# Layer normalisation moved from VectorE to ScalarE, turns of three dense layers reordered, gate softmax once per layer

## The reference, cut to what matters

```python
def _layernorm(x, axis=-1, eps=1e-05):
    m = jnp.mean(x, axis=axis, keepdims=True)
    v = jnp.var(x, axis=axis, keepdims=True)
    return (x - m) / jnp.sqrt(v + eps)

x = x + 0.5 * _L0_ffn_ref(_layernorm(x), ...)     # 128 -> 64 channels -> relu of 16 per channel -> 64 -> 128
x = x + _L0_attn_ref(_layernorm(x), ...)          # 16 heads of 8, rotary, causal
x = x + 0.5 * _L0_ffn_ref(_layernorm(x), ...)
x = x + 0.5 * _L1_ffn_ref(_layernorm(x), ...)     # gate softmax over 8 experts, each takes its top 128 rows
x = x + _L1_attn_ref(_layernorm(x), ...)          # gated recurrence over the 512 rows
x = x + 0.5 * _L1_ffn_ref(_layernorm(x), ...)
```

## Time and profile before

| | us |
|---|---|
| median of 3 runs (lowest to highest) | 1874.82 (1872.78 to 1875.02) |
| the profiled execution, its own time | 1875.22 |
| its span in the trace | 1873.2 |
| busy: PE / DVE / ACT / POOL | 1581.5 / 1360.9 / 1089.0 / 760.4 |
| granted TensorE clock, mean | 0.915 |
| query layer, from its first statistics at | 20.0 |
| attention, first maximum and last score product | 273.6 to 894.5 |
| gate layer, first statistics to last probabilities | 907.9 to 1063.0 |
| scan layer, first statistics to last probabilities | 1399.3 to 1536.3 |
| experts (both), first and last selection matrix | 1123.5, 1864.2 |

### The profile page before, as it was taken

How to read it: one execution, slowest core, us unless ns; L and a number is a source line. 1 busy time by engine, 2 the same in 40 slices (tenths; PEclk the granted TensorE clock), 3 DMA queues, 4 the chain that set the end, 5 groups by cost and what they waited for, 6 DMA issues and landing times. The chain is left out here.

```text
span 1873.2 us, 39185 instructions
## 1 busy us (share of the span) xinstructions
PE 1581.5 (84%) x11698; PEld 1107.9 (59%) x11698; DVE 1360.9 (73%) x3422; ACT 1089.0 (58%) x2225; POOL 760.4 (41%) x1170
## 2 busy tenths in 40 slices
PE   4878749999999999998699529999977751999998
PEld 1444424555555555554355329999964531999997
DVE  4898746777777777774388668777768976777776
ACT  2444313666666666666466427787755531877876
POOL 1565542333333333333233256665401212666540
PEclk9989856999999999999899759999988875999999
DMA  5111231111111111110011301111000110121110
GB/s 135 31 38 50 59 105 36 43 43 42 41 41 41 44 39 42 40 35 2 1 34 33 110 19 39 38 34 29 25 1 23 34 34 12 39 60 46 43 48 23
DMA packets 72819, 76.39 MB, mean 41 GB/s; under 512 B 13040, under 2 KB 61488, under 8 KB 72752
## 3 DMA queue, kind: packets, MB, share of 16 engines
q1 hardware_dynamic: 64560, 58.77, 10.9%
q0 software_dynamic: 8192, 16.79, 3.4%
HBM read 51.40 MB, written 24.12 MB: 40 GB/s over the span
## 5 line engine op out<-in xcount | busy, mean ns | idle before, releaser
L951 DVE TENSOR_REDUCE at_negmax<-at_s_ps 128x2 f32<-128x1024 f32 (+3 forms) x384 | 394.5, 1045 | 174.9 <-PE at_s_ps L741 170.4
L862 ACT ACTIVATE at_p<-at_x_ps 128x512 f32<-128x512 f32 x640 | 353.5, 591 | 224.1 <-PE at_x_ps L751 221.3
L918 POOL TENSOR_SCALAR_AFFINE_SELECT at_p<-at_p 128x256 f32<-128x256 f32 (+1 forms) x448 | 190.7, 438 | 354.9 <-ACT at_p L862 354.9
L1175 POOL DMA_INDIRECT e_x_in<-xn,e_row_c x256 | 258.5, 1010 | 145.7 <-POOL e_row_c L1171 103.5
L739 PE MATMUL at_s_ps<-at_kr,at_qr 72*128 72x512 bf16 (+3 forms) x1024 | 253.0, 312 | 20.6 <-DMA at_kr<-k_parts 18.2
L751 PE MATMUL at_x_ps<-at_qr,at_kr 74*128 74x512 bf16 (+3 forms) x1024 | 236.4, 306 | 23.0 <-ACT at_p L862 12.9
L1296 DVE TENSOR_TENSOR e_hid_lo<-e_hid,e_hid_hi 128x512 fp32r<-128x512 f32 x256 | 177.2, 693 | 85.3 <-ACT e_hid_hi L1260 85.3
L741 PE MATMUL at_s_ps<-maskb,identb 128*128 128x128 bf16 x1024 | 202.1, 225 | 0.0
L1259 ACT ACTIVATE e_hid<-e_h_ps 128x512 f32<-128x512 f32 x256 | 155.0, 605 | 39.4 <-PE e_h_ps L1201 38.9
L766 PE MATMUL at_o_ps<-at_p,at_va 128*32 128x512 f32 (+3 forms) x2048 | 157.0, 449 | 1.6 <-POOL at_p L918 1.6
L1201 PE MATMUL e_h_ps<-e_x_hi,w_hi 128*128 128x256 f32 x512 | 156.0, 305 | 0.1
(11 more groups left out here) (184 smaller groups left out, 3515.2 us busy)
## 6 DMA issues: line engine op xcount, KB each, us to landing
at_qr<-q_parts SPq DMA_DIRECT2D x192, 96.0 KB
k_parts<-m_kparts SPq DMA_DIRECT2D x48, 96.0 KB
at_kr<-k_parts SPq DMA_DIRECT2D x64, 72.0 KB
xres<-in_x_dram SPq DMA_DIRECT2D x8, 512.0 KB, 7.3
xn<-m_n_xhat SPq DMA_DIRECT2D x16, 256.0 KB, 2.3
e_x_in<-xn,e_row_c POOLq DMA_INDIRECT x256, 2.5
xn<-sc_n_xhat SPq DMA_DIRECT2D x16, 256.0 KB, 2.3
out_dram<-xres SPq DMA_DIRECT2D x16, 256.0 KB, 2.3
```

Of the source, the lines that this page charges most:

```text
L862: a.activation(p_sb[g % 2][:, i, :], x_ps[i % 2][:], ACT.Exp, scale=SCALE).then_inc(x_read, 1)
L918: sel = gp.affine_select(out=part, in_=part, compare_op=ALU.is_ge, fill=0.0, base=0, pattern=[[0, n] for n in part.shape[1:-1]] + [[1, P]] ...
L951: v.tensor_reduce(negmax[u][:, h0:h0 + len(heads), c], s_ps[k % 2][:, 0:len(heads) * pitch].rearrange("p (j w) -> p j w", w=pitch)[:, :, 0:w],
L1175: nc.gpsimd.indirect_dma_start(out=x_in[k][u][:], out_offset=None, in_=xn_dram, in_offset=bass.IndirectOffsetOnAxis(ap=row_c[k][:, u:u + 1 ...
```

## The change

1. `Norm.apply` moves from DVE to ACT: `Identity` with scale and bias columns. For the bias POOL multiplies the negated mean (`less`, made by DVE) by the reciprocal deviation (`shift`), behind the power.
2. The pipeline has a fourth stage, `ahead`: statistics, power and shift of norm 1 are made one turn before the head that uses them. `widen` waits until the last pair's normalised rows are done, since the columns have one buffer. In the query and gate layers ACT does norm 1 first in the head's turn; in the scan layer last in the turn before.
3. The turns of the gate and the scan layer are reordered on every engine; the scan layer is written out in full (`unrolled`), with two buffers for `ts`. In the gate layer `g_ps` and `xt2_ps` use other banks, and `HV["gate"]` goes from 3 to 5, so that DVE makes five hidden rows of eight.
4. DVE only copies the scores of a pair (`keep`); maximum, difference, exponential, sum, reciprocal and product are made once at the end of the layer over all 64 groups of 8.

```diff
-HV = {"qkv": 5, "gate": 3}
+HV = {"qkv": 5, "gate": 5}
...
+    def widen(self, dve, i):
+        after(dve, self.xhat_done, i * W)
         dve.wait_ge(self.mv_done, i + 1)
-        v.tensor_scalar(self.vare[:], self.mv[:, :, 1], EPS, None, ALU.add).then_inc(self.var_done, 1)
+        dve.sem_inc(self.dve_turn, 1)
+        self.nc.vector.tensor_scalar(self.less[:], self.mv[:, :, 0], -1.0, None, ALU.mult)
+        self.nc.vector.tensor_scalar(self.vare[:], self.mv[:, :, 1], EPS, None, ALU.add).then_inc(self.var_done, 1)
...
+        pool.wait_ge(self.rstd_done, i + 1)
+        pool.sem_inc(self.pool_turn, 1)
+        self.nc.gpsimd.tensor_tensor(self.shift[:], self.less[:], self.rstd[:], ALU.mult).then_inc(self.shift_done, 1)
+
+    def apply(self, act, i):
+        act.wait_ge(self.shift_done, i + 1)
         for b in range(W):
             for c in range(C):
                 j = b * C + c
-                s = self.nc.vector.tensor_scalar(
+                s = self.nc.scalar.activation(
                     self.xhat[b][:, c * D:(c + 1) * D], self.xres[:, i * W + b, c * D:(c + 1) * D],
-                    self.mv[:, j, 0:1], self.rstd[:, j:j + 1], ALU.subtract, ALU.mult)
+                    ACT.Identity, bias=self.shift[:, j:j + 1], scale=self.rstd[:, j:j + 1])
             s.then_inc(self.xhat_done, 1)
...
+    def keep(self, dve, i):
+        dve.wait_ge(self.scored, (i + 1) * W)
+        self.nc.vector.tensor_copy(self.probs[:, :, bass.ds(i * W * E, W * E)].rearrange("p c (b e) -> p b c e", b=W),
+                                   self.bank[:, 0:W * C * E].rearrange("p (b c e) -> p b c e", b=W, c=C)).then_inc(self.read, 1)
...
+        dve.wait_ge(self.read, TURNS)
+        v.tensor_reduce(self.mx[:], self.each, AX.X, ALU.max).then_inc(self.maxed, 1)
+        dve.wait_ge(self.maxed, 1)
+        v.tensor_tensor(self.each, self.each, self.mx[:].unsqueeze(2).to_broadcast([P, C * NB, E]), ALU.subtract).then_inc(self.lessened, 1)
+        dve.wait_ge(self.exp_done, 1)
+        v.tensor_reduce(self.den[:], self.each, AX.X, ALU.add).then_inc(self.summed, 1)
...
+    turn(0, None, None, None)
+    turn(1, 0, None, None)
+    turn(2, 1, 0, None)
+    turn(3, 2, 1, 0)
+    with eng.Fori(0, TURNS - 4) as r:
+        turn(r + 4, r + 3, r + 2, r + 1)
+    turn(None, TURNS - 1, TURNS - 2, TURNS - 3)
+    turn(None, None, TURNS - 1, TURNS - 2)
+    turn(None, None, None, TURNS - 1)
...
-        g_ps = xt_ps[0]
+        g_ps = xt_ps[0] if qkv else r_ps[1]
         y_ps = [r_ps[3], r_ps[0]]
+        xt2_ps = s_ps if qkv else y_ps
...
+                def turn_gate(ahead, head, middle, tail):
+                    if middle is not None:
+                        channels(middle)
+                    if tail is not None and not is_first(tail):
+                        score(tail - 1)
+                    if head is not None:
+                        turn_first(head)
+                    if middle is not None:
+                        output(middle, tail)
+                    if head is not None:
+                        project_in(head)
+                    if tail is not None:
+                        if middle is not None:
+                            pe.wait_ge(x_added, middle * W + W)
+                        turn_second(tail)
...
+                def turn(ahead, head, middle, tail):
+                    if head is not None:
+                        norm1.apply(act, head)
+                    if qkv and tail is not None:
+                        norm2.apply(act, tail)
                     if middle is not None:
                         act.wait_ge(hid_used, (middle + 1) * HT)
                         a.activation(g_t[:], g_ps[:], ACT.Identity, bias=gbias).then_inc(g_read, 1)
...
```

More of the change, by code:

```diff
@@ new lines, in project_in, with score, turn_qkv @@
+                def project_in(head):
+                    for b in range(W):
+                        pe.wait_ge(xt_read, head * W + b + 1)
+                        pe.matmul(s_ps[b][:], h["win2"][:], xhat_t[b][:], start=True, stop=True).then_inc(s_full, 1)
+                def score(tail):
+                    pe.wait_ge(xt2_read, tail * W + W)
+                    for b in range(W):
+                        gate.tensor(pe, tail, b, xhat2_t[b])
+                def turn_qkv(ahead, head, middle, tail):
@@ L410, in turn @@
                     if middle is not None:
                         channels(middle)
-                        if not qkv:
-                            output(middle, tail)
                     if tail is not None:
-                        for b in range(W):
-                            pe.wait_ge(norm2.xhat_done, tail * W + b + 1)
-                            transpose_chunks(pe, s_ps[b], norm2.xhat[b], h["ident"]).then_inc(xt2_full, 1)
-                    if qkv and middle is not None:
+                        turn_second(tail)
@@ L461, in split @@
                             a.activation(r["parts"][:, 1, :], r["b"][:], ACT.Copy).then_inc(p2_done, 1)
-                def turn(head, middle, tail):
-                    if not qkv and tail is not None and not is_first(tail):
-                        gate.scalar(act, tail - 1)
+                def turn(ahead, head, middle, tail):
[3 more added lines that the diff above has]
+                        norm2.apply(act, tail)
                     if middle is not None:
@@ L469, in turn @@
                         a.activation(g_t[:], g_ps[:], ACT.Identity, bias=gbias).then_inc(g_read, 1)
-                    if qkv and tail is not None and not is_first(tail):
-                        split(tail - 1, LATE)
-                    if tail is not None:
-                        for b in range(W):
-                            act.wait_ge(xt2_full, tail * W + b + 1)
-                            a.activation(xhat2_t[b][:], s_ps[b][:], ACT.Copy).then_inc(xt2_read, 1)
+                    if qkv and tail is not None:
+                        if not is_first(tail):
+                            split(tail - 1, LATE)
+                        copy_second(tail)
                     if head is not None:
@@ L479, in turn @@
                             a.activation(xhat_t[b][:], xt_ps[b][:], ACT.Copy).then_inc(xt_read, 1)
+                    if not qkv and tail is not None:
+                        for b in range(W):
+                            after(act, xn_out[b], tail * 16)
+                        norm2.apply(act, tail)
                     if head is not None:
@@ L490, in turn, with copy_second @@
                         split(tail, EARLY)
+                    if not qkv and tail is not None:
+                        after(act, gate.scored, tail * W)
+                        copy_second(tail)
+                def copy_second(tail):
+                    for b in range(W):
+                        act.wait_ge(xt2_full, tail * W + b + 1)
+                        a.activation(xhat2_t[b][:], xt2_ps[b][:], ACT.Copy).then_inc(xt2_read, 1)
                 pipeline(act, turn)
@@ L1374, in _, with turn @@
             def _(pe):
-                def turn(head, middle, tail):
+                def turn(ahead, head, middle, tail):
+                    if head is not None:
+                        for b in range(W):
+                            pe.wait_ge(norm1.xhat_done, head * W + b + 1)
+                            transpose_chunks(pe, xt_ps[b], norm1.xhat[b], h["ident"]).then_inc(xt_full, 1)
                     if middle is not None:
@@ L1414, in _, with turn @@
                 a = nc.scalar
-                def turn(head, middle, tail):
-                    if tail is not None and not is_first(tail):
-                        gate.scalar(act, tail - 1)
+                def turn(ahead, head, middle, tail):
+                    if head is not None:
+                        for b in range(W):
+                            act.wait_ge(xt_full, head * W + b + 1)
+                            a.activation(xhat_t[b][:], xt_ps[b][:], ACT.Copy).then_inc(xt_read, 1)
                     if middle is not None:
```

248 lines of the change are left out of this document (108 added, 140 removed).

## The result

| | before | after |
|---|---|---|
| median, us | 1873.98 (1872.78 to 1875.02) | 1897.22 (1895.04 to 1901.17) |
| ratio to before | | 1.0127 [1.0106, 1.0147] |
| profiled execution: own time, span | 1875.22, 1873.2 | 1895.04, 1893.3 |
| query layer, first statistics to last value copy | 234.6 | 237.1 |
| gate layer, first statistics to end of softmax | 155.1 | 161.4 |

The change costs 23 us where I forecast 3; 1897.2 lies just above my range. I take layer lengths from DVE's timeline.

A forecast was written before the change was run, and what follows sets the result against it. Bounds: query turn by norm 2's chain through DVE and PE, changed gate and scan turns by ACT. Query -1.4, gate +3.6, scan +0.5 sum to +2.7: span 1875.9, own time 1877.9, median 1877.5 us; range 1857 to 1896.

The forecast's parts named there:

- The price of a piece and of the shift: Normalised pieces on ACT: 0.385 us each in a row, 3.2 us per eight; POOL's shift 0.4 us with its wait.
- relief: Rival, all three layers: pieces on ACT overlap down to 0.25 us, norm 2 is ready earlier, 1853 us; chance 0.20.
- ACT is the bound everywhere: Rival, all three layers: pieces on ACT do not overlap, 0.48 us each, 1901 us; chance 0.12.
- the second turn gives half back: Query layer start: 0.7 us longer, with the first norm going from 2.14 to 3.6 us and half regained in turn two.
- the turn hangs on norm 2: Query layer: PE waits for norm 2's second sequence, ready at 9.3 us; steady turn 27.4 us, change 0.
- PE will wait for DVE's sixth hidden row: Gate layer, input copy to next channel copy: PE waits for that row, no more for ACT's tenth; about 10.5 us.
- Two edits act against each other: Gate layer: five hidden rows on DVE against norm 2's group on ACT; turn from 16.5 to 16.9 us.
- low-clock rival: Gate layer: PE's clock falls in a new gap of about 2.2 us, 3.4 us a turn, 1895 us; chance 0.15.
- the 15 that I had named as a sign of being wrong: Scan layer: turns over 15 us would show the forecast wrong.
- 13.3 us, for 15.36 now: Scan layer: ACT's work per turn sums to 13.3 us, so four turns change by -2.06 us each.
- two sigmoids with waits 1.8: Scan layer: term of ACT's 13.3 us turn, 1.8 us for two sigmoids and their waits.
- the second pair's norm 1 ahead of the first gates: Scan layer start: ACT does this norm (3.2 us) first; part of +3.4 us up to the third pair's residual addition.

The follow-up runs named there:

- the split: Kernel before with the changed query layer, norm 2's second sequence on DVE: 1874.55 us; under the gate layer, the same in the changed gate layer: 1872.59 us.
- the filled run: Kernel before with the changed scan layer alone, PE's waits filled with products nobody reads: 1880.10 us, 1.0036.
- the combined query turn: Gate layer of before; changed query layer, norm 2's second sequence on DVE, five filling products; scan layer reordered, filled, norm 2 split: 1850.91 us, 0.9875.

## Why the prediction was wrong

**The price of a piece and of the shift: right.** Eight pieces in 3.18 us (3.2), shift 0.38 with its wait (0.4). The rivals "relief" and "ACT is the bound everywhere" are out. The Trainium skill's rule that products and sums belong on VectorE ("ScalarE: Activation LUTs", "Rules for kernel authors") is right for the piece, 0.40 against 0.27 us. It doesn't tell where the pieces should go in the scan layer: in the changed order DVE gave 1892 and ACT 1888 us, with intervals that overlap.

**Query layer: turn right (27.34 for 27.4), ends wrong: +2.5 for -1.4.** The step that failed is "the second turn gives half back". The first hidden rows come 1.6 us later, the second turn's 2.6, the third's 3.7: the second input copy of the first turn waits 1.02 us for PE's projection (3.62 us long), 0.28 before (2.91 us), and norm 2's first group is ready 12.8 us behind the second turn's hidden rows, 11.8 before (it waits 1.51 us for its shift on ACT). The last two turns gave back 0.6, not 2.1. This is read from the traces; no run tests it. That the turn hangs on norm 2 was half the truth: the split shows that it hangs on norm 2, on the transposes and on the clock behind it.

**Gate layer: +6.3 for +3.6.** The start +0.3 for -0.9 (the first addition comes 3.0 us later, and the two turns behind it give back 2.6), the turns 17.23 for 16.9 (five times 0.7, +3.5 for +2.0), and what is left for the end, +2.5, as forecast. The part with ACT's norm-2 group was exact (6.42 for 6.4), and the split confirms that it holds the turn. The rest of the turn, for which I wrote "PE will wait for DVE's sixth hidden row", was 10.8 us for 10.5; and the step "Two edits act against each other" failed: five rows on DVE are no relief but a second loss, for with three the turn is 0.4 us shorter. The low-clock rival did not come about here: the granted clock is 1.00.

**Scan layer: +13.1 for +0.5, the main miss.** Up to the third addition +8.1 for +3.4; four turns -3.3 for -8.2; the turn without norm 1 +4.1 for +0.7; the end +4.3 for +4.6. Turns of 15.04 us on average are over the 15 that I had named as a sign of being wrong. The step that failed is "13.3 us, for 15.36 now": the sum of ACT's work was right (13.39 with the clock held), but I wrote "two sigmoids with waits 1.8" with gates at full clock. I had the rival, a low clock after new waits of PE, with a mechanism and 0.15, but tied it to the gate layer and did not ask the same of the scan layer, where the earlier trace rows showed 0.77 and 0.89 already. There PE had 11 us of work in my 13.3 us turn. And the length of one wait does not decide, as that rival had it: the clock fell behind waits of 1.10 and 0.62 us, and held behind 1.66. The filling puts the clock's part at 9.4 us of the layer. With the clock held (the filled run against the kernel before) the terms are +6.9, -7.9, +0.2 and +4.7, so three of the four come near my forecast and the rest of the error is the start, +6.9 for +3.4: I counted the second pair's norm 1 ahead of the first gates, and missed that the third pair's statistics stand behind the first recurrence on DVE (4.4 us at the third addition).

So 1895, the rival's number, was close to the result by another layer: luck, and not a hit of that rival.

Left open: why the last scan turn is longer in some orders (11.7 to 14.4 us in the filled ones), which of the split and the shorter filling gives the combined query turn its gain, and the 0.4 us of attention.

## What to carry to other kernels

When work is taken from the engine that is full, redo the turn with the clock that PE will have in the new gaps: a low clock that was hidden before can surface, and here it cost 9.4 us in one layer. Filling PE's waits with unread products is a cheap test of it, and a remedy where the filling fits the wait; in the kernel before it cost more in the query layer (5.3 us) than it gave in the scan layer (3.2). Split a group that stands on the path between two engines rather than move it whole, and in the turns that fill the pipeline look for statistics that stand behind a wait.

## What the runs showed of the hardware

Useless products made the scan layer 9.4 us shorter (granted clock 0.78 to 0.88, then 1.00). PE's clock fell in the scan turn after waits of 1.10 and 0.62 us with 2.5 us of work between them, while in the gate layer waits of 0.61 and 1.21 us left it at 1.00: the length of one wait does not tell it. A float32 product of 128x512 with a 128x128 weight took 0.89 us at full clock in a row. And an operand that was ready earlier did not shorten the turn in proportion: in the split query turn 1.5 us gave 0.3, while the output behind it ran at the 1.2 GHz level.
